# Linear attention with a butterfly FFN: k^T (x | 1) by groups of 256 features in place of x^T k with separate key sums, all keys as max(z, -b) on VectorE, first loads in smaller pieces

## The chip, the cores and the metric

The kernel runs on one core of a Trainium2 chip. The metric is device time in microseconds, from the runs of the whole program. One execution was also recorded by the hardware profiler; all rows below come from it.

## The reference, cut to what matters

```python
# x: (4, 1024, 128), W_qkv: (128, 3072), 16 heads of 64 features
q, k, v = split(x @ W_qkv)                    # each (4, 16, 1024, 64)
q = relu(q @ W_f + b_f);  k = relu(k @ W_f + b_f)
kv    = einsum('bhnd,bhne->bhde', k, v)       # sum over tokens
out   = einsum('bhnd,bhde->bhne', q, kv)
norm  = einsum('bhnd,bhd->bhn', q, k.sum(tokens))
x = layernorm(x + (out / (norm + 1e-6)) @ W_out + b_out)
h = butterfly(x @ W_exp + b_exp, up_weights)  # 512 hidden, 9 stages of 2x2 blocks
h = butterfly(gelu(h + up_bias), down_weights)
x = layernorm(x + h @ W_con + b_con + down_bias)
```

## The kernel before, in words

W_f is folded into the query and key weights and W_v into W_out, per head; the two butterflies are multiplied into W_exp and W_con once, on GpSimd and VectorE. Because v is linear in x, the sum of k v over tokens is W_v applied to the sum of k x. So the kernel never forms v: it accumulates x^T k (128 by 1024, in two PSUM banks, `kx_ps`) over the 8 token tiles of a batch, and `head_maps` (L763) turns that into one 128 by 128 map for each pair of heads.

Many products are split in high and low parts (`split`, L654): three matmuls of the type fp32r in place of one. Plain fp32 matmuls run in two passes each, so each appears as two weight loads and two matmuls in the trace.

The order of all work is written by hand in 43 slots. Every engine has one program, a loop over the slots (TensorE L879, ScalarE L1111, VectorE L1415), and waits only on semaphores. In slots 0 to 3 two token tiles are projected to keys, after that one a slot, with two query steps of 512 tokens by 128 features, and from slot 11 two steps of attention, then the up and down products of the FFN. Key and query results go through a ring of three PSUM banks (`take_ring`, L667): a bank is written again once its result has been read out.

The work around the change:
- Keys: `project_k` (L699) makes a token tile's keys in two halves of 512 features. For batches 0 and 1 a fourth matmul adds the bias row, and ScalarE reads the bank out as relu (`k_relu`, L1015). For batches 2 and 3 (`BARE`) the bias is left out, VectorE stores max(z, -b) (`k_max`, L1268), and what is missing, b times the sum over tokens, is added back at the end of a batch (`kx_end`, L1280, and `ksum_mask`, L1303). Every slot's VectorE program has the first half's eviction near its start, the second half's behind normalisation and the low parts.
- kx: `add_kx` (L727) multiplies a tile of x (weights) with its 1024 keys (moving), two fp32 matmuls of 512 columns.
- Key sums: VectorE adds the key tiles into `k_total` (`k_sum`, L1291), and `ksum` (L741) multiplies them with a column of ones, eight fp32 matmuls with one moving column, once per batch.
- The start: SP loads half of batch 0's x, the key weights in two halves, and waits for the second half before it issues more (L455 to L465). TensorE transposes weights, folds W_f (`fold_wf`, L684), ScalarE and VectorE take high and low part.
- The down butterfly on VectorE (`down_step`, L1205): two products and a sum per stage, with its coefficients loaded by SP (`load_down`, L476). The up butterfly on GpSimd (`up_step`, L573, `load_up`, L470). A load waits until the step before last has read its buffer, and everything behind it in SP's queue waits too. The bias's butterfly (`bias_row_step`, L1227) is on VectorE in slots 10 to 13, and the finished down weights are transposed in slot 13 (`ffn_weights`, L861).

Of the kernel before, what the change touches and what calls it, by code (L numbers as in the profile page):

```python
# [5 lines left out]
def postln_linear_attention_butterfly_ffn_kernel(  # L6
# [23 lines left out]

    fp32 = mybir.dt.float32
    fp32r = mybir.dt.float32r
    ALU = mybir.AluOpType
# [16 lines left out]
    ALLT = BATCH * TILES  # L50
    NORM_EPS = 1e-6
# [41 lines left out]
    KX_SLOT = {TILES * b + FIRST + 1: b for b in range(BATCH)}  # L93
# [7 lines left out]
    for b in range(BATCH):  # L101
        MAPS_SLOT[TILES * b + ATTN_AT - 2] = (b, 0)
        MAPS_SLOT[TILES * b + ATTN_AT] = (b, 1)
    XT_SLOT = {}
    for b in range(1, BATCH):
        XT_SLOT[TILES * (b - 1) + 2] = (b, 0)
        XT_SLOT[TILES * (b - 1) + 6] = (b, 1)
# [27 lines left out]
    DOWN_STEP_SLOT = {1: 0, 2: 1, 3: 2, 5: 3, 6: 4, 7: 5, 8: 6, 9: 7, 12: 8}  # L135
    PS_STEP = 3
    PS_LAST = 7

    BIAS_SLOT = {10: [0, 1], 11: [2, 3], 12: [4, 5], 13: [6]}
    BIAS_T_SLOT = 14  # L140
# [26 lines left out]

    BARE = 2 * TILES
    k_taken, taken = {}, {}
    for use in ring_of:  # L170
        if use[0] == "k" and use[1] >= BARE:
            k_taken[use] = len(k_taken) + 1
        else:
            taken[use] = len(taken) + 1
# [3 lines left out]
    desk_of = {("wq",): 0, ("wcon",): 1, ("v", 0): 2, ("v", 1): 3}  # L178
    WCON_SLOT = 0
    V_SLOT = {1: 0, 2: 1}  # L180
    for s in range(SLOTS):
        order = []
        if s in KSUM_SLOT:
            order.append(("ksum", KSUM_SLOT[s]))
        if s in ATT_T_SLOT:
            order.append(("attn", ATT_T_SLOT[s]))
        if s in MAPS_SLOT:
            order.append(("maps", *MAPS_SLOT[s]))
# [4 lines left out]
        if s == WDN_SLOT:  # L193
            order.append(("wdn",))
# [9 lines left out]
    spare_of = {}  # L204
# [13 lines left out]
    with ctx:  # L218
# [20 lines left out]
        ones = sb("ones", [128, 1])  # L239
# [3 lines left out]
        bf_h = sb("bf_h", [128, D], fp32r)  # L243
        bf_rows = sb("bf_rows", [128, CH], fp32r)
        ones_r = sb("ones_r", [128, 128], fp32r)
# [11 lines left out]
        xs = [sb(f"xs{i}", [128, TILES, C]) for i in range(XBUF)]  # L257
# [4 lines left out]
        k_total = sb("k_total", [128, HD])  # L262

        m_whole = k_total[:, :].rearrange("p (a c) -> p a c", a=PAIRS)
# [50 lines left out]
        bias_row_term = x1_flat[0:HT, 2 * CH:2 * CH + 256].rearrange("p (f n) -> p f n", f=2)  # L315
# [9 lines left out]
        s_wk = [sem(f"k_weights_half_{n}_loaded") for n in range(2)]  # L325
# [8 lines left out]
        s_xs0 = sem("first_half_of_xs_0_loaded")  # L334
# [10 lines left out]
        s_bfz = sem("bf_rows_zeroed")  # L345
        s_bfh = sem("bf_hi")
        s_bfl = sem("bf_lo")
# [6 lines left out]
        s_voa = sem("vo_copied_act")  # L354
        s_vod = sem("vo_copied_dve")
        s_xp = sem("first_x_transposed")
        s_xTh = sem("xT_hi")
# [3 lines left out]
        s_ktaken = sem("ring_bank_of_bare_k_taken")  # L361
# [15 lines left out]
        s_ks = sem("k_summed")  # L377
        s_kxt = sem("kx_half_added")
        s_kxc = sem("kx_copied")
# [36 lines left out]
        def k_summed(eng, b, t):  # L416

            eng.wait_ge(s_ks, b * (TILES - 1) + max(t, 1))

# [21 lines left out]
        def _(sp):  # L441
# [7 lines left out]
            def load_x(b, chunks, done):  # L449
                dst = xs[b][:, :, :].rearrange("p (h t) c -> p h t c", h=CHUNKS)  # L450
                sp.dma_start(dst[:, chunks, :, :], xs_view[b, :, chunks, :, :]).then_inc(done, 16)
# [32 lines left out]
            load_x(1, slice(0, CHUNKS), s_xs[1])  # L484
# [46 lines left out]
            load_down(6)  # L531
            load_down(7)
            spread(0)
# [19 lines left out]
        def _(pool):  # L553
# [6 lines left out]
            g.memset(ones_r[:, :].bitcast(fp32), 1.0)  # L560
            g.memset(bf_rows[:, :].bitcast(fp32), 0.0).then_inc(s_bfz, 1)
            g.memset(ones[:, :], 1.0)
# [43 lines left out]

            pool.wait_ge(s_wffn, 32)
            for n in range(STAGES):
                up_step(n)
            for s in range(SLOTS):  # L610
# [12 lines left out]
                if s == NO_KEYS + 2:  # L623

                    pool.wait_ge(s_kxt, 2 * TILES * BATCH)
                    last = xs[(BATCH - 1) % XBUF][:, (CHUNKS - 1) * QUADS:CHUNKS * QUADS, :]
# [19 lines left out]
        def _(pe):  # L646
# [33 lines left out]
            def transpose_weights(grp, dst):  # L680
                pe.wait_ge([s_wq, s_wq, *s_wk, s_wv, s_wv][grp], 16)
                return transpose_tiles(dst, lambda i: wqkv_raw[:, (grp * 4 + i) * 128:(grp * 4 + i + 1) * 128])

            def fold_wf(grp, dst):  # L684
                for i in range(4):
                    col = (grp * 4 + i) * 128
# [4 lines left out]
            def fold_vo(n, dst):  # L691
# [5 lines left out]
                last.then_inc(s_fold, 1)  # L697

            def project_k(kt, half):  # L699
                b, t = kt // TILES, kt % TILES  # L700
                if half == 0 and t % QUADS == 0:
# [858 lines left out]
```

## Time and profile before

| | |
|---|---|
| median of 3 runs | 328.9 us (328.84 to 331.87) |
| the profiled execution's own time | 328.99 us |
| its span, first to last instruction | 327.2 us |
| TensorE matmul busy | 311.2 us, 95% |
| VectorE busy | 249.9 us, 76% |
| ScalarE busy | 156.3 us, 48% |
| GpSimd busy | 97.1 us, 30% |
| mean granted TensorE clock | 0.991 |
| first key projection | 9.64 us |
| first key projection of slot 4 | 43.13 us |

Matmuls are pipelined and their ends are modelled, so a matmul's listed duration holds time that it shares with the next one. What a matmul costs in a stream is the step from its start to the next start. A granted clock of 1.00 is 2.4 GHz.

### The profile page before, as it was taken

How to read it: one execution, taken by the hardware profiler on the slowest of the kernel's cores; microseconds unless marked ns; L12 is line 12 of the kernel's file. 1: busy time of each engine (PE TensorE's matmuls, PEld its weight loads, DVE VectorE, ACT ScalarE, POOL GpSimd, SP SyncE). 2: the span in 40 equal slices, each digit the busy share in tenths (PEclk: the TensorE clock that was granted, in tenths of full speed). 3: DMA queues.
4: the chain of work that ended last, by engine and by line, in shares of the span. 5: the costliest groups of instructions: out<-in, count | busy, mean ns of one | idle time of the engine just before them, and what ended most of it. 6: DMA issues, size and time to landing. Idle time of an engine off the chain costs nothing.

```text
span 327.2 us, 5512 instructions
## 1 busy us (share of the span) xinstructions
PE 311.2 (95%) x2009; PEld 234.4 (72%) x2009; DVE 249.9 (76%) x501; ACT 156.3 (48%) x279; POOL 97.1 (30%) x83
## 2 busy tenths in 40 slices
PE   5999999999999899999999999999999799999893
PEld 4766677767766677667768777776797587669793
DVE  3579989978989779888890997579838953758844
ACT  3634436535733343654461556346647846431442
POOL 4059999970000002400210122002302312423513
PEclk9999999999999989999999999999999999999998
DMA  4993425556705700370064002900190174372001
GB/s 140 311 327 128 134 75 184 189 201 148 175 2 136 151 0 2 103 160 0 5 156 105 0 35 68 195 0 32 20 229 16 36 167 94 93 159 75 1 34 64
DMA packets 19762, 33.95 MB, mean 104 GB/s; under 512 B 3960, under 2 KB 6680, under 8 KB 19736
## 3 DMA queue, kind: packets, MB, share of 16 engines
q1 hardware_dynamic: 19432, 33.54, 38.9%
q8 instruction: 16, 0.26, 0.3%
q10 hardware_dynamic: 304, 0.07, 0.1%
q14 instruction: 10, 0.08, 0.1%
HBM read 31.24 MB, written 2.36 MB: 103 GB/s over the span
## 4 chain that ended last, share of the span: by engine, by line
PE 76%; DVE 14%; issue 4%; ACT 2%; DMA 1%; POOL 1%; SPq 0%; POOLq 0%; DVEq 0%; ACTq 0%
PE ring L651 28%; PE kx_ps L738 14%; PE spare_ps L841 7%; PE attn_ps L651 7%; PE ring L758 4%; PE desk L772 3%; DVE qn L1335 2%; PE desk L660 2%; PE ring L718 2%; PE desk L747 2%; DVE k_total L1301 1%; DVE qn_l L1203 1%; DVE stats L1344 1%; DMA q<-in_L_attn_W_qkv_dram 1%; DVE k L1275 1%
## 5 line engine op out<-in xcount | busy, mean ns | idle before, releaser
L599 POOL TENSOR_TENSOR rstd<-var_eps,minus_half 128x4 f32<-128x4 f32 x14 | 19.3, 1381 | 176.9 <-DVE var_eps L1350 176.9
L1029 ACT ACTIVATE q<-ring,bf_col 128x512 f32<-128x512 f32 x64 | 43.9, 685 | 46.4 <-PE ring L651 45.6
L738 PE MATMUL kx_ps<-k,xs 128*128 128x512 f32 x128 | 60.3, 594 | 0.0
L1335 DVE TENSOR_TENSOR qn<-q,recips 128x512 f32<-128x512 f32 x64 | 43.5, 719 | 2.8 <-DMA recips<-recip_rows 2.8
L1013 ACT ACTIVATE qn_h<-qn 128x512 fp32r<-128x512 f32 x48 | 29.5, 625 | 27.5 <-DVE qn L1335 27.5
L582 POOL TENSOR_TENSOR y<-hid,y_up 128x512 f32<-128x512 f32 x18 | 32.8, 1843 | 15.9 <-DMA hid<-in_L_ffn_up_weights_dram 14.9
L738 PEld LDWEIGHTS kx_ps<-k,xs 128*128 128x128 f32 x128 | 24.2, 191 | 18.0 <-issue 15.4
L1301 DVE TENSOR_TENSOR k_total<-k_total,k 128x1024 f32<-128x1024 f32 x24 | 36.5, 1520 | 0.5 <-ACT k L1020 0.3
L1203 DVE TENSOR_TENSOR qn_l<-qn,qn_h 128x512 fp32r<-128x512 f32 x48 | 33.4, 704 | 2.9 <-ACT qn_h L1013 2.7
L651 PE MATMUL ring<-xT_h,wq_h 128*128 128x512 f32 x64 | 35.6, 556 | 0.0
L1275 DVE TENSOR_TENSOR k<-ring,bf_minus 128x512 f32<-128x512 f32 x32 | 21.9, 685 | 13.7 <-PE ring L651 13.7
L651 PE MATMUL ring<-wk_h,xT_h 128*128 128x512 f32 x64 | 29.6, 463 | 0.5 <-issue 0.5
L1092 ACT ACTIVATE hid<-ring,bup_col 128x512 f32<-128x512 f32 x28 | 19.2, 686 | 22.6 <-PE ring L651 22.5
L1020 ACT ACTIVATE k<-ring 128x512 f32<-128x512 f32 x32 | 19.1, 597 | 18.1 <-PE ring L718 18.1
L841 PE MATMUL spare_ps<-wdn,hid 128*128 128x128 f32 x224 | 26.7, 276 | 0.0
L841 PEld LDWEIGHTS spare_ps<-wdn,hid 128*128 128x128 f32 x224 | 26.0, 192 | 1.0 <-issue 0.8
L651 PE MATMUL ring<-wk_h,xT_l 128*128 128x512 f32 x64 | 25.5, 399 | 0.0
L651 PE MATMUL ring<-wk_l,xT_h 128*128 128x512 f32 x64 | 25.5, 399 | 0.0
L651 PE MATMUL ring<-xT_h,wq_l 128*128 128x512 f32 x64 | 25.4, 398 | 0.0
L651 PE MATMUL ring<-xT_l,wq_h 128*128 128x512 f32 x64 | 25.4, 397 | 0.0
L595 POOL TENSOR_TENSOR y<-x,rows 128x512 f32<-128x512 f32 (+1 forms) x9 | 14.9, 1657 | 22.6 <-ACT x L1083 17.1
L651 PE MATMUL attn_ps<-qn_h,m_h 128*128 128x512 f32 x48 | 19.9, 414 | 0.3 <-DVE qn_l L1203 0.3
(174 smaller groups left out, 580.6 us busy)
## 6 DMA issues: line engine op xcount, KB each, us to landing
recips<-recip_rows SPq DMA_DIRECT2D x64, 256.0 KB, 5.4
hid<-in_L_ffn_up_weights_dram SPq DMA_DIRECT2D x9, 512.0 KB, 4.2
x<-_L_ffn_down_weights_dram SPq DMA_DIRECT2D x9, 512.0 KB, 6.7
out_dram<-y SPq DMA_DIRECT2D x7, 256.0 KB, 2.0
xs<-in_L_attn_x_dram SPq DMA_DIRECT2D x3, 512.0 KB, 6.1
q<-in_L_attn_W_qkv_dram SPq DMA_DIRECT2D x2, 512.0 KB, 4.5
xs<-in_L_attn_x_dram SPq DMA_DIRECT2D x2, 256.0 KB, 2.7
q<-in_L_attn_W_qkv_dram SPq DMA_DIRECT2D x2, 256.0 KB, 3.9
```

What stands on the lines that cost most here:

```text
L582: g.tensor_tensor(term_up[f].rearrange("p (hi j lo) -> p hi j lo", j=2, lo=lo), w[:, :, :, :, f], yv[:, :, f:f + 1, :].to_broadcast([128, ...
L599: g.tensor_tensor(rstd[i][:, :], var_eps[i][:, :], minus_half[:, :].to_broadcast([128, QUADS]), ALU.pow).then_inc(s_rs[i], 1)
L651: last = t_.matmul(dst, lhsT, rhs, start=start and n == 0, stop=stop and n == len(pairs) - 1)
L738: t_.matmul(kx_ps[half], xs[b % XBUF][:, t, :], k[kt % KRING][:, half * CH:(half + 1) * CH], start=t == 0, stop=t == TILES - 1).then_inc(s ...
L841: last = t_.matmul(dst, hid[:, j, i * 128:(i + 1) * 128], wdn[:, j, :], start=j == 0, stop=j == HT - 1)
L1013: a_.activation(dst, src, ACT.Copy).then_inc(done, 1)
L1029: a_.activation(q[:, i % QRING, :], bank(("q", i))[:, :], ACT.Relu, bias=bf_col[:, :])\
L1092: a_.activation(hid[:, i, :], bank(("up", f))[:, :], ACT.Gelu, bias=bup_col[:, i:i + 1])\
L1203: v.tensor_tensor(dst, src, high.bitcast(fp32), ALU.subtract).then_inc(done, 1)
L1275: v.tensor_tensor(k[kt % KRING][:, half * CH:(half + 1) * CH].rearrange("p (h d) -> p h d", d=D), bank(("k", kt, half))[:, :].rearrange("p ...
L1301: v.tensor_tensor(k_total[:, :], k_total[:, :], k[kt % KRING][:, :], ALU.add).then_inc(s_ks, 1)
L1335: v.tensor_tensor(qn[:, a % NRING, :], q[:, a % QRING, :], recips[:, a % PAIRS // RC, a % RC, :], ALU.mult).then_inc(s_qn, 1)
```

## The change

- kx turns round. A key unit is no longer a token tile with 1024 features but a group of 256 features for a chunk of four token tiles; a half is two of these tiles. `project_k` makes it in twelve matmuls of 256 columns where six of 512 stood, without the bias matmul for any batch. `add_kx` uses the keys as weights and a tile of x with a 129th column of ones as the moving side: eight fp32 matmuls of 129 columns per unit. The sums over tokens of the keys come out in the 129th column. `k_sum`, `k_total` and `ksum` go.
- A finished group is copied by ScalarE (`kx_copy(b, g)`, sixteen times 128 by 258), TensorE transposes it back in halves of a batch (`transpose_kx`), and `kx_end` adds the bias term per half.
- VectorE evicts all keys as max(z, -b); ScalarE evicts none. The sum over x is taken for all batches; for batch 0 VectorE sums the first x banks, and the first `add_kx` waits for that sum.
- The second chunk of a batch's x^T is needed earlier; its transposes move.
- First loads: half of batch 0's first x chunk, 256 key features, the other half of x; SP waits for the 256 features, then loads the rest of the keys' weights in two pieces. Other x loads are issued per chunk. The later `load_up`, `load_down` and x loads change their order.
- The bias's butterfly moves from VectorE to GpSimd, behind the up butterfly. Several PSUM copies move from VectorE to ScalarE. The down steps move to slots 5 to 12, the first spread over slots 2 to 4.

```diff
+    KXE_SLOT = {(TILES * b + 2 * g - 1 if b else g + 2): (b, g) for b in range(BATCH) for g in range(GROUPS)}
+    KXT_SLOT = {FIRST: (0, 0), FIRST + 2: (0, 1), TILES + FIRST: (1, 0), TILES + 6: (1, 1)}
+    for b in range(2, BATCH):
+        KXT_SLOT[TILES * b + 2] = (b, 0)
+        KXT_SLOT[TILES * b + 6] = (b, 1)
...
-    DOWN_STEP_SLOT = {1: 0, 2: 1, 3: 2, 5: 3, 6: 4, 7: 5, 8: 6, 9: 7, 12: 8}
+    DOWN_STEP_SLOT = {n + 4: n for n in range(1, STAGES)}
...
-            load_x(0, slice(0, 1), s_xs0)
-            for half in range(2):
-                cols = slice(HD + half * CH, HD + (half + 1) * CH)
-                sp.dma_start(wqkv_raw[:, cols], W_qkv[:, cols]).then_inc(s_wk[half], 16)
-
-            sp.wait_ge(s_wk[1], 16)
-            load_x(0, slice(1, 2), s_xs[0])
+            sp.dma_start(xs[0][:, 0:2, 0:C], xs_view[0, :, 0, 0:2, :]).then_inc(s_xs0[0], 16)
+            load_wk(0, slice(HD, HD + 256))
+            sp.dma_start(xs[0][:, 2:4, 0:C], xs_view[0, :, 0, 2:4, :]).then_inc(s_xs0[1], 16)
+
+            sp.wait_ge(s_wk[0], 16)
+            load_x(0, [1], s_xs[0])
+            load_wk(1, slice(HD + 256, HD + CH))
+            load_wk(2, slice(HD + CH, HD + 2 * CH))
...
             load_up(2)
             load_up(3)
+            load_up(4)
+            load_up(5)
+            for b in range(2, BATCH):
+                load_x(b, range(CHUNKS), s_xs[b])
             load_down(2)
-            load_up(4)
-            load_down(3)
-            load_up(5)
             load_up(6)
-            load_down(4)
             load_up(7)
             load_up(8)
-            for b in range(2, BATCH):
-                load_x(b, slice(0, CHUNKS), s_xs[b])
+            load_down(3)
+            load_down(4)
             load_down(5)
             load_down(6)
+            spread(0)
             load_down(7)
-            spread(0)
             load_down(8)
...
+            for b in range(XBUF):
+                g.memset(xs[b][:, :, C:C1], 1.0).then_inc(s_xones, 1)
...
+            pool.wait_ge(s_up, 3 * STAGES)
+            for st in range(LOCAL):
+                bias_row_step(st)
...
             def project_k(kt, half):
...
+                cols = slice(g * 256, (g + 1) * 256)
+                for i in range(2):
+                    t = QUADS * c + 2 * half + i
+                    tok = slice(t * 128, (t + 1) * 128)
+                    last = split(bank(("k", kt, half))[:, i * 256:(i + 1) * 256],
+                                 (xT_h[:, b % 2, tok], xT_l[:, b % 2, tok]), (wk_h[:, cols], wk_l[:, cols]))
+                last.then_inc(s_made, 1)
...
             def add_kx(kt):
...
+                b, g, c = kt // TILES, kt % TILES // 2, kt % 2
+                if kt == 0:
+                    pe.wait_ge(s_xones, XBUF)
+
+                    pe.wait_ge(s_xpart, 1)
...
+                if c == 0 and GROUPS * b + g >= 2:
+                    pe.wait_ge(s_kxe, GROUPS * b + g - 1)
                 emptied(pe, ("k", kt, 1))
                 for half in range(2):
-                    t_.matmul(kx_ps[half], xs[b % XBUF][:, t, :], k[kt % KRING][:, half * CH:(half + 1) * CH],
-                              start=t == 0, stop=t == TILES - 1).then_inc(s_kxt, 1)
-
-            def ksum(b):
...
+                    for i in range(2):
+                        for j in range(2):
+                            col = half * CH + i * 256 + j * 128
+
+                            last = t_.matmul(kx_ps[g % 2][:, j * C1:(j + 1) * C1], k[kt % KRING][:, col:col + 128],
+                                             xs[b % XBUF][:, QUADS * c + 2 * half + i, :],
+                                             start=c == 0 and half == 0 and i == 0 and j == 0,
+                                             stop=c == 1 and half == 1 and i == 1 and j == 1)
+                    last.then_inc(s_kxt, 1)
+
+            def transpose_kx(b, half):
+                take_desk(("kxT", b, half))
+                pe.wait_ge(s_kxe, GROUPS * b + 2 * half + 2)
+                transpose_tiles(desk, lambda i: kxT_pairs[:, 4 * half + i, 0:C]).then_inc(s_dmade, 1)
...
-            def kx_copy(b):
-                act.wait_ge(s_kxt, 2 * TILES * (b + 1))
+            def kx_copy(b, g):
+                act.wait_ge(s_kxt, 2 * (TILES * b + 2 * (g + 1)))
...
+                if s == 0:
+                    w_lo(2, wk_l[:, 256:CH], wk_h[:, 256:CH])
...
+                for kt in k_tiles(s)[1:]:
+                    k_max(kt, 0)
+                if s == 0:
+                    v.reduce_sum(x_part[:, 0, 1:2], desk[:, :], axis=mybir.AxisListType.X).then_inc(s_dtaken, 1)
+                    v.reduce_sum(x_part[:, 0, 0:1], kx_both[:, :].rearrange("p (a n) -> p a n", a=2)[:, :, 0:256],
+                                 axis=mybir.AxisListType.XY).then_inc(s_xpart, 1)
```

## Rows read from the trace of the kernel before

**Rows 1.** The page: busy us, share of the span, instructions of an engine.
```profile
PE 311.2 (95%) x2009; PEld 234.4 (72%) x2009; DVE 249.9 (76%) x501; ACT 156.3 (48%) x279; POOL 97.1 (30%) x83
```
**Rows 2.** Stretches (start:end, length): busy us of engines, granted clock, DMA share, GB/s.
```profile
0.00:9.60 9.60, 5.26 (x28) 4.30 (x28) 3.87 (x5) 4.06 (x8) 3.54 (x16) 1.00 0.54 168
9.60:43.10 33.50, 33.46 (x143) 23.36 (x144) 27.06 (x20) 14.17 (x25) 22.74 (x12) 1.00 0.70 209
43.10:80.30 37.20, 37.20 (x218) 26.54 (x216) 33.10 (x29) 18.12 (x31) 27.66 (x16) 1.00 0.51 163
80.30:112.00 31.70, 30.19 (x196) 21.76 (x195) 27.39 (x53) 14.64 (x25) 0.00 (x0) 1.00 0.56 127
112.00:180.00 68.00, 67.37 (x426) 49.66 (x426) 53.24 (x102) 31.51 (x56) 8.68 (x8) 0.97 0.28 65
252.00:311.00 59.00, 55.27 (x445) 43.92 (x446) 41.96 (x131) 27.82 (x49) 19.59 (x16) 1.00 0.36 87
```
**Rows 3.** Chain of waits in order of time: start, us, what.
```profile
1.65 4.34 DMA q<-in_L_attn_W_qkv_dram
...
6.04 1.12 PE ring L660 x4
7.15 1.03 PE attn_ps L687 x8
8.19 0.91 PE spare_ps L687 x8
...
9.64 0.94 PE ring L651 x3
...
12.30 0.44 PE desk L660 x4
...
41.76 0.86 PE attn_ps L695 x4
...
56.08 1.68 PE desk L747 x16
...
71.94 1.72 PE kx_ps L738 x4
73.66 1.41 PE ring L651 x6
...
173.33 3.57 PE spare_ps L841 x32
```
**Rows 4.** Groups of instructions: line, form, count, busy us, mean ns, idle before.
```profile
L738 PE MATMUL kx_ps<-k,xs 128*128 128x512 f32 x128 | 60.3, 594 | 0.0
```
**Rows 5.** Timeline of TensorE in the last chunk's up products: start, us, instruction.
```profile
313.50 0.28 PE L651 MATMUL ring<-x1T_l,wup_h 128*128 128x256 f32 x1
...
314.33 0.27 PE L651 MATMUL ring<-x1T_h,wup_l 128*128 128x256 f32 x1
```
**Rows 6.** Timeline of TensorE at the end of slot 13.
```profile
110.07 1.95 PE L747 MATMUL desk<-ones,k_total 128*128 128x1 f32 x16 [1.51 <-DVE wdn L1480]
...
113.54 0.63 PE L651 MATMUL ring<-wk_h,xT_h 128*128 128x512 f32 x1
...
115.68 0.63 PE L651 MATMUL attn_ps<-qn_h,m_l 128*128 128x512 f32 x1
```
**Rows 7.** Groups of VectorE: key sums, evictions of keys, terms of down steps.
```profile
L1301 DVE TENSOR_TENSOR k_total<-k_total,k 128x1024 f32<-128x1024 f32 x24 | 36.5, 1520 | 0.5 <-ACT k L1020 0.3
...
L1275 DVE TENSOR_TENSOR k<-ring,bf_minus 128x512 f32<-128x512 f32 x32 | 21.9, 685 | 13.7 <-PE ring L651 13.7
...
L1221 DVE TENSOR_TENSOR late<-x,spare_ps 128x512 f32<-128x512 f32 x7 | 6.2, 907 | 2.1 <-DMA x<-_L_ffn_down_weights_dram 2.1
```
**Rows 8.** Timeline of SP's queue: issue of the last two up loads.
```profile
53.95 6.00 SPq L474 DMA_DIRECT2D hid<-in_L_ffn_up_weights_dram  x2
```
**Rows 9.** DMA issues: queue, count, KB each, median us to landing.
```profile
x<-_L_ffn_down_weights_dram SPq DMA_DIRECT2D x9, 512.0 KB, 6.7
```

More of the change, by code:

```diff
@@ L102, in postln_linear_attention_butterfly_ffn_kernel @@
         MAPS_SLOT[TILES * b + ATTN_AT - 2] = (b, 0)
[L103 to L107, printed above, removed]
+        MAPS_SLOT[TILES * b + ATTN_AT - (0 if b else 1)] = (b, 1)
+    XT_SLOT = {2: (1, 0), 3: (1, 1), 8: (2, 0), 11: (2, 1)}
+    for b in range(3, BATCH):
+        XT_SLOT[TILES * b - 6] = (b, 0)
+        XT_SLOT[TILES * b - 5] = (b, 1)
     ATTN_LAST = [ATTN_AT + (PAIRS // 2) * (n + 1) - 1 for n in range(ALLCH)]
@@ L255, in postln_linear_attention_butterfly_ffn_kernel @@
         minus_half = sb("minus_half", [128, 1])
-        xs = [sb(f"xs{i}", [128, TILES, C]) for i in range(XBUF)]
+        xs = [sb(f"xs{i}", [128, TILES, C1]) for i in range(XBUF)]
         xT_h = sb("xT_h", [128, 2, N], fp32r)
@@ L323, in postln_linear_attention_butterfly_ffn_kernel @@
         desk = pb("desk")
-        s_wk = [sem(f"k_weights_half_{n}_loaded") for n in range(2)]
+        s_wk = [sem(f"k_weights_part_{n}_loaded") for n in range(3)]
         s_wq = sem("q_weights_loaded")
@@ L333, in postln_linear_attention_butterfly_ffn_kernel @@
         s_xs = [sem(f"xs_{b}_loaded") for b in range(BATCH)]
-        s_xs0 = sem("first_half_of_xs_0_loaded")
+        s_xs0 = [sem(f"tiles_of_xs_0_part_{n}_loaded") for n in range(2)]
+        s_xones = sem("x_ones_made")
         s_wffn = sem("ffn_weights_loaded")
@@ L483, in _ @@
             load_down(0)
-            load_x(1, slice(0, CHUNKS), s_xs[1])
+            load_x(1, range(CHUNKS), s_xs[1])
             for h in range(2):
@@ L678, in take_half, with transpose_weights, fold_wf @@
                     pe.wait_ge(s_dn, 3 * STAGES)
[L680 to L686, printed above, removed]
+            def transpose_weights(first, n, dst):
+                for i in range(n):
+                    last = t_.transpose(dst[:, i * 128:(i + 1) * 128], wqkv_raw[:, (first + i) * 128:(first + i + 1) * 128],
+                                        ident[:, :])
+                return last
+            def fold_wf(first, n, dst):
+                for i in range(n):
+                    col = (first + i) * 128
                     last = t_.matmul(dst[:, i * 128:(i + 1) * 128], wT[:, col:col + 128], wf_diag[:, :],
@@ L716, in project_k @@
-                if kt == 0 and half == 0:
-                    pe.wait_ge(s_bfl, 1)
-                t_.matmul(dst, ones_r[:, :], bf_rows[:, :], start=False, stop=True).then_inc(s_made, 1)
+                b, g, c = kt // TILES, kt % TILES // 2, kt % 2
+                if kt < 2:
+                    if kt == 0 and half == 0:
+                        pe.wait_ge(s_x01h, 1)
+                        pe.wait_ge(s_x01l, 1)
+                    else:
+                        pe.wait_ge(s_xTh, c + 1)
+                        pe.wait_ge(s_xTl, c + 1)
+                elif g == 0 and half == 0:
+                    pe.wait_ge(s_xTh, CHUNKS * b + c + 1)
+                    pe.wait_ge(*half_taken(("x", b, c)))
@@ L1415, in _ @@
             for s in range(SLOTS):
                 if s in KSUM_SLOT:
-                    if s == min(KSUM_SLOT):
-                        dve.wait_ge(s_const, 7)
                     ksum_mask(KSUM_SLOT[s])
-                if s in KX_SLOT and TILES * KX_SLOT[s] >= BARE:
-                    kx_end(KX_SLOT[s])
                 for kt in k_tiles(s)[:1]:
-                    if kt >= BARE:
-                        k_max(kt, 0)
+                    k_max(kt, 0)
                 if s == 0:
-                    for half, fold in enumerate([spare_ps, attn_ps]):
-                        cols = slice(half * CH, (half + 1) * CH)
-                        dve.wait_ge(s_wh, 3 + half)
-                        lo(wq_l[:, cols], fold[:, :], wq_h[:, cols], s_wl)
+                    dve.wait_ge(s_xTh, 2)
```

529 lines of the change are left out of this document (256 added, 273 removed).

## The prediction

> **What bounds the kernel now.** I read the busy times first: TensorE 311.2 of 327.2 us, VectorE 249.9 [rows 1]. A busy share says little while matmuls overlap, so the next view is the table of stretches [rows 2]. The reader is to see where TensorE is idle: 4.3 us of the first 9.6, next to nothing from 9.6 to 80.3 (33.46 of 33.50, 37.20 of 37.20), 1.5 us in 80.3 to 112, 3.7 us near the end. So from the first key projection at 9.64 on, time is what TensorE's instructions cost, and what they cost net is read from the chain of waits, where a piece's length is its step to the next [rows 3]: six split matmuls of 512 columns 1.41 us (0.235 each), a token tile's four kx passes 1.72 (0.43 a pass), sixteen ksum passes 1.68, thirty-two passes of 128 columns in the down product 3.57 (0.112 a pass), four transposes 0.44.
>
> **TensorE, part by part.** (Minus is faster.)
> 1. Bias matmuls of batches 0 and 1 go: 16 tiles x 2 halves x 0.235 [rows 3] = -7.5.
> 2. ksum goes, once per batch: 4 x 1.68 [rows 3] = -6.7.
> 3. kx turns round. Before, a tile has 4 passes, 128 in all [rows 4], 1.72 a tile. After, each of the 32 key units has 8 matmuls in two passes, 16 passes, with keys as weights and 129 columns moving. No row has 129 columns. Below, the bound is ksum's pass, which moves one column: 1.68/16 = 0.105, so 1.68 a unit and -1.3 in all; above, it is the vo fold's pass of 256 columns, 0.86/4 = 0.215 [rows 3], so 3.44 a unit and +55. The nearest row by far is 128 columns: 0.1116 x 129/128 x 16 = 1.80. I take 32 x (1.80 - 1.72) = +2.6.
> The Trainium skill speaks against this edit: TensorE: Matmul & The Clock Gate, section Back-to-back issue gap, gives about 81 ns per weight-load and matmul pair at 128 columns and 131 ns at 512. By that, 32 x (16 x 81 - 4 x 131) ns is an estimated +24.7, and the sum below would be about 343. The trace disagrees: its 512-column pass takes 3.9 times its 128-column pass (0.43 against 0.112), so cutting it into four costs little.
> 4. Key projections become halves of 256 columns. The last chunk's up products have that form: 7 steps from 313.50 to 314.33 [rows 5], 0.1186 each, so 12 x 0.1186 = 1.42 against 6 x 0.235 = 1.41: +0.4 over 32 units.
> 5. kx must be transposed back, eight times four transposes: 8 x 0.44 [rows 3] = +3.5.
> TensorE together: -7.7.
>
> **The start.** The weights' second half is what the first projection hangs on: its transfer ends at 5.99 (1.65 + 4.34), then come four transposes (1.12), folds (1.03 and 0.91 for eight passes) and the copies, till 9.64 [rows 3]. After, 256 KB stand ahead of the first transposes and folds where 768 KB stood. The landing is between a third of 4.34 us and all of it, so 3.1 to 5.99; I take half, 3.8, and 2.8 us more for two transposes, four fold passes and half-size copies, so a first projection near 6.6: -3.0. It is not all won. Six weight tiles are folded later, among the projections: 6 x 0.11 + 12 x 0.112 = +2.0. And the first add_kx now waits for VectorE's sum over x, because it overwrites the bank that is summed: behind the first projection VectorE has seven instructions in order (three key evictions, two low parts, two sums), each about 0.69 by [rows 7] (the 256-wide one less), some 4.8 us plus about one for its own waits. TensorE has only three projections, ten transposes and four fold passes meanwhile, 3.7 us, so it waits about +2.0. Start together: +1.0, between -1.0 (no such wait) and +4 (the landing no earlier either, 3.0 lost).
>
> **Slot 13.** Here the kernel has its one hole in mid-course. VectorE brings the down weights late, TensorE idles 1.51 us before ksum, and then matmuls step at 0.43 (five steps from 113.54 to 115.68) [rows 6] instead of 0.235, in the stretch with a mean granted clock of 0.97 [rows 2], so part of it at 1.2 GHz, the lower of the two levels. Seven such steps cost 1.4. ksum is gone, the weights go through another bank and ScalarE copies them, the bias rows leave VectorE. I take the hole as gone: -2.9 (0 if another wait takes its place).
>
> **VectorE, and what covers it.** It loses 28 key sums; the 24 in [rows 7] are 36.5 us. It gains 32 more evictions, as the 32 there, 21.9 us, and four half-size kx_end more. In 80.3 to 112, where normalising has begun, it is busy 27.39 of 31.70 us [rows 2]; two more butterfly steps land there (each two terms of 0.9 and a sum) and four evictions, while bias rows, a copy and three key sums go. So it stays about as full, and TensorE may run ahead by three ring banks. What fails first if that cover goes is the second key eviction: it stands behind two normalisations and the butterfly term, and the next slot's first query projection needs its bank. I give such waits +1.0, from 0 to +6 (the rival below).
> ScalarE gives up 32 evictions and takes sixteen small kx copies and some others: it stays about half idle [rows 2], at nothing. GpSimd's bias rows start after the up butterfly and are due only in slot 13: nothing, and if late, TensorE waits there. On SP's queue the two later x loads move ahead and the down weights' loads behind; more and smaller issues cost it under half a us each, covered everywhere but at the start, which is in the start's bounds.
>
> **Sum.** The profiled execution took 328.99 us (span 327.2), which is 0.1 from the median of the three runs, 328.9. -7.7 + 1.0 - 2.9 + 1.0 = -8.6, so 320.4 us. Its own range runs from 317 (the -1.0 start, no waits in VectorE) to 325 (hole replaced, or start at its worse end).
>
> **Rival 1, slower: short kx passes cost more than the down product's.** The 512 passes of 129 columns are odd in count and every second result starts 129 numbers into its bank. Each ns per pass is 0.51 us. It decides from 8.6 + 3.3 us, 23 ns a pass (0.135 instead of 0.1125), to be slower by over 1%; at half of the way to the 256-column row, 0.164, it gives 347 us. Against it: passes of 128 columns and of one differ by 7 ns only, so weights and columns overlap well. Chance 0.10.
> The skill's page PSUM — Partial Sum Buffer, section Specifications (TRN2), names 8-byte cachelines and a significant slowdown for outputs that are not contiguous; these are contiguous but half of them begin inside such a line, which no row here shows.
>
> **Rival 2, little change: the wait moves to VectorE.** Every key now leaves through an engine that works in order, and butterfly step 3 stands among the evictions of slot 7. Its weights are loaded after the last up weights, whose issue waits for GpSimd and ends at 59.95 [rows 8]; a down load of 512 KB takes 6.7 us to land [rows 9], so 67. Slot 7 would begin near 59 and the term be due near 61: VectorE, and soon TensorE, would wait up to 6 us. A second such load, step 7, waits behind the first reciprocals' spread. That and a hole that stays give 320.4 + 5 + 1.5 = 327. For it: the order in the queue is fixed. Against it: GpSimd should get through faster once the key sums, two SBUF operands each, no longer run beside it. Chance 0.22.
>
> **Rival 3, faster: the start comes through whole.** No wait on the x sum, halves landing at a third, no waits in VectorE: 320.4 - 2 - 1 - 0.7 = 316.7. It needs the loads to gain what their size promises; the first loads are smaller but also more. Chance 0.13.
>
> **Numbers.** Forecast 0.55, rivals 0.10, 0.22, 0.13. Within 1% is what a measurement of this kernel can't tell from no change: 325.6 to 332.2. Faster takes the forecast, rival 3 and a small part of rival 2: 0.71. Same takes most of rival 2: 0.18. Slower, rival 1 and a little more: 0.11. The range 316 to 328.5 leaves out rival 1, the worst of 2 and the far end of 3.
>
> **What would show it.** Right: 512 kx passes at about 0.112 us; key projections in 12 steps of 0.119; no ksum and bias matmuls; first projection near 6.6 but slot 4 (43.1 before) only one or two us earlier; no hole at slot 13 and a clock of 1.00 there; after slot 20 the same distances as before, since in batches 2 and 3 ksum's 1.68 is paid back by 0.6 for kx and 0.9 for transposes. Wrong: kx passes above 0.13, or TensorE idle in slots 5 to 12 with VectorE waiting for a down load, or the first add_kx late by more than the 2 us.

## The result, and the profile after

The changed kernel takes 325.33 us in the median (323.96 to 326.08) where the kernel before takes 329.0 beside it (328.84 to 331.87): a ratio of 0.986, 95% interval 0.981 to 0.990. A second set of runs gave 323.36 against 329.81, 0.983 (0.978 to 0.988). The forecast was 320.4. So the sign was right and some 2 to 5 us of the 8.6 did not arrive (3.7 came in the first set, 6.45 in the second). The profiled execution took 323.96 us, the fastest of its four and 5.0 less than the profiled one of before; everything below that compares the two traces accounts for these 5.0.

The page of the changed kernel, first line (answers [rows 1]):

```profile
PE 302.8 (94%) x2521; PEld 268.2 (83%) x2521; DVE 218.7 (68%) x492; ACT 142.6 (44%) x267; POOL 96.0 (30%) x105
```

TensorE lost 8.4 us of busy time and VectorE 31. The table of stretches of the changed kernel, columns as in [rows 2], says where TensorE was idle instead:

```profile
0.00:9.60 9.60, 4.77 (x20) 3.93 (x21) 3.78 (x6) 2.66 (x6) 3.04 (x17) 1.00 0.59 171
9.60:43.10 33.50, 31.87 (x262) 31.29 (x262) 17.39 (x27) 8.99 (x17) 21.20 (x15) 1.00 0.75 212
43.10:80.30 37.20, 37.04 (x330) 34.17 (x329) 30.30 (x40) 12.60 (x23) 28.39 (x33) 1.00 0.42 138
80.30:112.00 31.70, 28.63 (x254) 25.29 (x253) 27.77 (x52) 12.25 (x23) 0.00 (x0) 1.00 0.65 155
112.00:180.00 68.00, 67.83 (x583) 60.93 (x582) 45.73 (x90) 34.43 (x64) 9.17 (x8) 1.00 0.29 66
```

The reader is to see two stretches. From 9.6 to 43.1 TensorE has 1.6 us idle where it had none; from 80.3 to 112 it has 3.1 where it had 1.5. The hole of slot 13 [rows 6] is gone: 112 to 180 is full (67.83 of 68.00) and its clock 1.00, not 0.97. The chain of waits of the changed kernel (start, us, what; answers [rows 3]) gives the second place, and the price of a kx unit:

```profile
37.45 1.79 PE kx_ps L770 x16
...
85.84 2.63 issue
88.47 0.93 PE attn_ps L671 x3
```

A kx unit of 16 passes takes 1.79, 0.112 a pass. TensorE stands idle for 2.63 us ahead of the first attention product, in slot 11. In the timeline further down, slot 4's first key projection comes at 44.36, where before it came at 43.13.

### The profile page after: what moved, and what is told of

It reads as the page before. It is cut to its first block, busy times and chain, and to the rows that moved or that the text cites. A ratio compares the mean times of both kernels' runs of the same rounds, so it can differ in the third digit from the quotient of the medians.

```text
span 322.1 us, 6555 instructions
## 1 busy us (share of the span) xinstructions
PE 302.8 (94%) x2521; PEld 268.2 (83%) x2521; DVE 218.7 (68%) x492; ACT 142.6 (44%) x267; POOL 96.0 (30%) x105
## 4 chain that ended last, share of the span: by engine, by line
PE 79%; DVE 8%; issue 5%; DMA 3%; ACT 2%; SPq 1%; POOL 1%; POOLq 0%; DVEq 0%; ACTq 0%
PE ring L671 30%; PE kx_ps L770 16%; PE attn_ps L671 9%; PE spare_ps L871 8%; PE ring L788 4%; PE desk L680 3%; PE desk L802 2%; DMA recips<-recip_rows 1%; PE attn_ps L709 1%; DVE qn L1375 1%; PE attn_ps L822 1%; DVE stats L1384 1%; DMA xs<-in_L_attn_x_dram 1%; DMA recip_rows<-recip 1%; PE attn_ps L828 1%
## 5 line engine op out<-in xcount | busy, mean ns | idle before, releaser
L1327 DVE TENSOR_TENSOR k<-ring,bf_minus 128x512 f32<-128x512 f32 x64 | 43.9, 687 | 46.6 <-PE ring L671 46.5
L770 PE MATMUL kx_ps<-xs,k 128*128 128x129 f32 x512 | 62.4, 275 | 1.6 <-issue 1.6
L770 PEld LDWEIGHTS kx_ps<-xs,k 128*128 128x128 f32 x512 | 61.1, 191 | 3.4 <-issue 1.8
L671 PE MATMUL ring<-wk_h,xT_h 128*128 128x256 f32 x128 | 39.3, 307 | 1.0 <-DVE wk_l L1265 1.0
L671 PE MATMUL ring<-wk_l,xT_h 128*128 128x256 f32 x128 | 36.4, 284 | 0.0
L671 PE MATMUL ring<-wk_h,xT_l 128*128 128x256 f32 x128 | 36.4, 284 | 0.0
L671 PE MATMUL ring<-xT_h,wq_h 128*128 128x512 f32 x64 | 27.7, 434 | 0.0
L671 PEld LDWEIGHTS ring<-wk_h,xT_h 128*128 128x128 f32 x128 | 24.8, 193 | 3.3 <-issue 1.6
L671 PEld LDWEIGHTS ring<-wk_l,xT_h 128*128 128x128 f32 x128 | 24.9, 194 | 1.6
L671 PEld LDWEIGHTS ring<-wk_h,xT_l 128*128 128x128 f32 x128 | 24.7, 193 | 0.0
```

Source lines behind the costliest of these rows:

```text
L671: last = t_.matmul(dst, lhsT, rhs, start=start and n == 0, stop=stop and n == len(pairs) - 1)
L770: last = t_.matmul(kx_ps[g % 2][:, j * C1:(j + 1) * C1], k[kt % KRING][:, col:col + 128], xs[b % XBUF][:, QUADS * c + 2 * half + i, :], st ...
L1327: v.tensor_tensor(k[kt % KRING][:, half * CH:(half + 1) * CH].rearrange("p (h d) -> p h d", d=D), bank(("k", kt, half))[:, :].rearrange("p ...
```

## Where the forecast's gain went, by position

The same work in both traces, changed minus before, worked out from the starts of the same matmuls in TensorE's timeline (slot 4: first key projection; slots 8, 12, 16: first matmul of the norm; end: the execution's own time). The forecast's column adds up its terms as far as that slot.

| | before | changed | difference | by the forecast |
|---|---|---|---|---|
| slot 4 | 43.13 | 44.36 | +1.2 | -2.1 |
| slot 8 | 68.17 | 66.47 | -1.7 | -4.4 |
| slot 12 | 94.18 | 95.06 | +0.9 | -5.0 |
| slot 16 | 126.84 | 123.33 | -3.5 | -8.3 |
| end | 328.99 | 323.96 | -5.0 | -8.6 |

Two stages fall short: up to slot 4 by 3.3 us, and from slot 8 to 12 by 3.2 (a gain of 0.6 was due, 2.6 were lost). The others are better than forecast (by 0.6, 1.1 and 1.2). In both short stages 0.44 us is not lost but moved: four transposes of x stand ahead of the mark in the changed kernel that stood behind it before (16 against 12 by slot 4, 24 against 20 by slot 12; 16 and 24 in both by slots 8 and 16). So the losses are 2.9 and 2.7 us, and the stages behind them are better by 0.2 and 0.7. The timeline of TensorE in the kernel before, at slot 12:

```profile
94.18 1.95 PE L758 MATMUL ring<-q,ksum_cols 128*32 128x128 f32 x64
```

The timeline of TensorE in the changed kernel (start, us, instruction, idle time before it) shows the first of the two places, and the marks of slots 4, 8 and 12:

```profile
5.45 1.06 PE L709 MATMUL attn_ps<-wf_diag,q 128*128 128x128 f32 x4
7.53 0.55 PE L671 MATMUL ring<-wk_h,xT_h 128*128 128x256 f32 x1 [1.02 <-DVE wk_l L1265]
7.88 0.42 PE L671 MATMUL ring<-wk_l,xT_h 128*128 128x256 f32 x1
8.10 0.42 PE L671 MATMUL ring<-wk_h,xT_l 128*128 128x256 f32 x1
...
12.27 0.28 PE L671 MATMUL ring<-wk_h,xT_h 128*128 128x256 f32 x1
12.39 0.28 PE L671 MATMUL ring<-wk_l,xT_h 128*128 128x256 f32 x1
...
16.00 2.02 PE L770 MATMUL kx_ps<-xs,k 128*128 128x129 f32 x16 [1.63 <-issue]
...
44.36 0.36 PE L671 MATMUL ring<-wk_h,xT_h 128*128 128x256 f32 x1
...
66.47 1.96 PE L788 MATMUL ring<-q,ksum_cols 128*32 128x128 f32 x64 [0.16 <-ACT q L1079]
...
83.84 1.09 PE L802 MATMUL desk<-vo,kx 128*64 128x128 f32 x16 [0.44 <-DVE m_l L1265]
...
95.06 1.95 PE L788 MATMUL ring<-q,ksum_cols 128*32 128x128 f32 x64
```

The first projection begins at 7.53, not at 6.6. From there matmuls step at 0.21 us until about 12, and then at 0.12 for the same shape. They take 1.8 times as long at first, as at the lower of TensorE's two levels (1.2 and 2.4 GHz), though the stretch's granted clock reads 1.00. And the first kx product comes after 1.63 us of idle time. The second place, on SP's queue and on VectorE:

```profile
55.43 17.17 SPq L481 DMA_DIRECT2D x<-_L_ffn_down_weights_dram  x4
72.65 1.82 SPq L502 DMA_DIRECT2D recip_rows<-recip  x4
```

```profile
68.80 0.95 DVE L1359 RECIPROCAL recip<-recip 128x128 f32<-128x128 f32 x1 [1.48 <-ACT recip L1117]
...
81.89 1.29 DVE L1375 TENSOR_TENSOR qn<-q,recips 128x512 f32<-128x512 f32 x2 [1.66 <-DMA recips<-recip_rows]
...
83.70 1.11 DVE L1284 TENSOR_TENSOR late<-x,spare_ps 128x512 f32<-128x512 f32 x1
...
86.53 1.11 DVE L1284 TENSOR_TENSOR attn_ps<-x,spare_ps 128x512 f32<-128x512 f32 x1
87.67 0.70 DVE L1294 TENSOR_TENSOR spare_ps<-late,attn_ps 128x512 f32<-128x512 f32 x1
```

The reciprocals are done at 69.7, but SP issues their spread at 72.65: the last of four down loads in front of it (step 6's) waits until step 4's terms have left its buffer. VectorE then idles 1.66 us for the spread, and after it has a slot's worth of work up to the sum of step 6 at 88.4. The first attention product waits for that sum, because step 6 keeps its second term in the attention bank. So there seem to be two causes in a row; the next experiments take them away one by one.

## Experiments: slot 11

The changed kernel ran again beside three variants.

> The changed kernel once more, unaltered, so that the three beside it have it on the same chip. Both theories: 324 to 326 us, a ratio of 0.983 to 0.991 to the kernel before; TensorE idle 2.6 us in slot 11 ahead of the first attention product, and the first key projections of 256 columns stepping at 0.21 us until about 12 us.

Measured: 323.36 us (323.26 to 324.36), a little below the 324 to 326 expected, with the idle time (2.64 us) in slot 11 and the slow first steps as expected. The variants of the next sections are compared with this run where nothing else is said.

**The bank.**

```diff
-    PS_LAST = 7
+    PS_LAST = 6
```

> Step 6 of the down butterfly keeps its second term in SBUF and not in the attention bank, so the first attention product waits for step 5 alone. Theory A (the 2.6 us hole of slot 11 is the wait for the attention bank, which VectorE frees late because step 6's terms and sum stand in slot 10 behind two normalisations, two low parts and an eviction): the first attention product starts by 86.0 instead of 88.5, the hole shrinks to under 0.6, the kernel is 2 to 2.6 us faster than the changed one. Theory B (the hole is the late spread of the reciprocals, which SP issues behind a down load): the product then waits for the low part of q instead, the hole stays above 1.5 and the time moves by less than 1 us.

Measured: 321.96 us (321.51 to 322.03), ratio 0.977 (0.973 to 0.982). The timeline of TensorE:

```profile
84.17 1.09 PE L802 MATMUL desk<-vo,kx 128*64 128x128 f32 x16 [0.32 <-DVE m_l L1265]
86.00 0.39 PE L671 MATMUL attn_ps<-qn_h,m_h 128*128 128x512 f32 x1
...
93.09 1.18 PE L788 MATMUL ring<-q,ksum_cols 128*32 128x128 f32 x35 [0.48 <-DVE k L1327]
```

The hole is gone and the product comes at 86.00 as theory A said, and the profiled executions differ by 2.3 us (322.03 and 324.36), but the medians by 1.4 and not by 2 to 2.6 (the slowest of its runs is still 1.2 below the fastest of the changed kernel's). VectorE is still late, and TensorE meets it again at 93.09.

**The spread.**

```diff
+        coef_dn.append(qn[:, 2:4, :].rearrange("p a n -> p (a n)"))
+        DN_BUF = [0, 1, 0, 1, 0, 1, 2, 1, 0]
...
-                if n >= 2:
+                if n >= 2 and n != 6:
                     sp.wait_ge(s_dn, 3 * n - 4)
```

> The down load of step 6 gets a coefficient buffer of its own and no wait, so the spread of the first reciprocals no longer stands behind it. It is issued near 70.0 instead of 72.65. Theory B (the late spread makes the hole): first normalisation at 80.2 instead of 81.9, hole under 0.6, 2.3 to 3 us faster than the changed kernel. Theory A (VectorE's order and the attention bank make it): VectorE gains the 1.7 us it idled ahead of the first normalisation, but the 6.5 us from there to the sum of step 6 stay, so about 1.0 to 1.5 us of hole stay and the gain is 1.3 to 2 us.

Measured: 322.37 us (322.08 to 322.87), ratio 0.979 (0.973 to 0.985). SP's queue, and the chain of waits:

```profile
70.14 1.73 SPq L504 DMA_DIRECT2D recip_rows<-recip  x4
```

```profile
85.62 1.38 issue
87.01 0.94 PE attn_ps L673 x3
```

The spread goes out at 70.14, VectorE no longer idles, and 1.38 us of the hole stay: theory A's 1.0 to 1.5. The gain, 1.0, is a little under its 1.3, and again no run overlaps with the changed kernel's.

**Both.**

> Only the two edits for slot 11 (step 6 out of the attention bank, and a coefficient buffer of its own for step 6 so that the spread goes out early). Theory A (each takes away one of two things in a row, so together they leave nothing to wait for): no idle time ahead of the first attention products, first one at 85.6 or earlier, 2.6 to 3.1 us less than the changed kernel, so 320.3 to 321 us. Theory B (they cure the same wait, and the bank alone already cured it): no better than the bank alone, 322 us.

Measured: 320.83 us (319.99 to 321.63), ratio 0.973 (0.969 to 0.978): 2.5 less than the changed kernel's 323.36, about the sum of the two alone (1.4 and 1.0). TensorE's timeline has the first attention product with no idle time before it:

```profile
85.33 0.40 PE L673 MATMUL attn_ps<-qn_h,m_h 128*128 128x512 f32 x1
```

Theory A holds: two causes in a row. The bank alone already takes away the wait ahead of this product, but only both edits leave VectorE nothing to be late with at slot 12 as well.

## Experiments: the start

**Idle transposes.**

```diff
             pe.wait_ge(s_const, 2)
+            idle_work(8)
             transpose_first_x(0)
...
+            idle_work(3)
             transpose_first_x(1)
...
             fold_wf(PAIRS, 2, attn_ps)
+            idle_work(5)
```

> Sixteen transposes of the identity into a bank not yet in use: eight before the first x tiles are there, three while the second piece of x is awaited, five behind the first folds. Nothing reads them. Theory A (the first key projections step at 0.21 us because TensorE had been idle between its first pieces of work and still ran at the lower clock): steps of 0.12 from the first projection at 7.5 on, slot 4's first projection 1.5 to 2.5 us earlier than 44.6, the kernel 1.5 to 2.5 us faster than the changed one. Theory B (the slow steps are the weight loads or the DMA traffic of the start): steps stay at 0.21 until about 12 us, and the time moves by less than 0.5 us.

Measured: 324.57 us (324.39 to 325.15), 1.2 slower than the changed kernel beside it in the median and the same in the profiled execution (324.39 and 324.36). Yet the steps are as theory A has them:

```profile
5.76 0.71 PE L903 MATMUL ring<-ident 128*128 128x128 f32 x5
6.95 0.35 PE L671 MATMUL ring<-wk_h,xT_h 128*128 128x256 f32 x1 [0.48 <-DVE wk_l L1272]
7.14 0.28 PE L671 MATMUL ring<-wk_l,xT_h 128*128 128x256 f32 x1
7.26 0.28 PE L671 MATMUL ring<-wk_h,xT_l 128*128 128x256 f32 x1
```

They step at 0.12 from the first unit on, and the norm of slot 8 begins at 64.47, not 66.87: 2.4 us won, 0.9 of it ahead of the first projection (6.95 for 7.83). The weight loads of these matmuls and the DMA traffic (163 GB/s in the first 9.6 us of both traces) are the same, so what made the steps slow is that TensorE had been idle. (The Trainium skill, TensorE: Matmul & The Clock Gate, section What's actually happening, gives 1.2 GHz as the state of an idle array and 2.4 GHz as that of a busy one; these two traces agree, 0.21 and 0.12 for 256 columns.) The chain of waits then shows the loss:

```profile
84.79 2.63 issue
87.43 1.62 PE attn_ps L671 x3
89.05 2.17 PE ring L671 x9
```

The hole of slot 11 is as long as before, and behind it three products take 1.62 and nine 2.17, where the changed kernel has 0.94 and 1.40. That stretch's granted clock is 0.95. So 1.4 us go there, and 1.0 to the store of the reciprocals, which took 3.74 us to land in this run and 2.73 in the other. All four runs have a lower mean clock (0.991 to 0.995) than the changed kernel's four (0.996 to 1.000). Why the store was late and why the clock fell stays open.

**The x sum.**

```diff
             lo(xT_l[:, 0, 0:256], kx_ps[0][:, 0:256], xT_h[:, 0, 0:256], s_x01l)
+            v.reduce_sum(x_quart[:, 0:1], kx_ps[0][:, 0:256], axis=X).then_inc(s_xquart, 1)
...
-                    pe.wait_ge(s_xpart, 1)
+                    pe.wait_ge(s_xquart, 1)
+                elif kt == 2:
+                    pe.wait_ge(s_xquart, 2)
```

> Only the x sum of batch 0 in two pieces, so that the first kx product waits for a sum taken long before. Theory A (the 1.63 us TensorE idles ahead of it are the wait for that sum): the first kx product starts near 14.4 instead of 16.0, slot 4 comes 1.6 us earlier, and the time is 0 to 1.6 us less than the changed kernel's 323.4, less than 1.6 if slot 11 takes it back as it did with the idle transposes. Theory B (it waits for the evicted keys): the idle time stays above 1 us.

Measured: 322.44 us (321.81 to 325.0), ratio 0.978 (0.971 to 0.986), so 0.9 us less than the changed kernel by the medians and 1.5 by the ratios, within the intervals. TensorE's idle time ahead of the first kx product is gone:

```profile
14.77 1.95 PE L773 MATMUL kx_ps<-xs,k 128*128 128x129 f32 x16
```

It starts right behind the transposes. These come 0.56 us later than in the first trace of the changed kernel (14.34 for 13.78), as the slow steps last until 12.8 here. Slot 4 comes at 43.11 instead of 44.36, and slot 11 keeps an idle 2.47. Theory A.

**The size of the first loads.**

```diff
-            sp.dma_start(xs[0][:, 0:2, 0:C], ...
-            load_wk(0, slice(HD, HD + 256))
-            sp.dma_start(xs[0][:, 2:4, 0:C], ...
+            sp.dma_start(xs[0][:, 0:4, 0:C], ...
+            load_wk(0, slice(HD, HD + CH))
...
-            load_wk(1, slice(HD + 256, HD + CH))
```

> The first half of batch 0's x in one load of 256 KB instead of two of 128, and the first 512 columns of the key weights in one load of 256 KB instead of two of 128; all else as changed. Theory A (the forecast's step: the first projection comes earlier because less has to land before it): the first projection starts 0.6 to 1.2 us later than 7.5. Theory B (what brought it forward is that two weight tiles are transposed and folded ahead of it, not eight, and the number of loads costs what their size saves): it starts within 0.3 us of 7.5, and the time stays within 0.5 us.

Measured: 325.61 us (324.48 to 325.99), ratio 0.986 (0.979 to 0.992). The chain of waits:

```profile
1.48 3.31 DMA q<-in_L_attn_W_qkv_dram
...
8.35 1.62 PE ring L669 x6
```

The weights' transfer ends at 4.79, and the first projection starts at 8.35: 0.8 later than 7.53, and later than in each trace with the small loads and no idle transposes (7.22 to 7.83). Theory A holds, for 0.8 of the 2.1 us by which the change brought the first projection forward from 9.64; the rest was not taken apart further. The edit makes both the first x load and the first weight load larger, so the two are not told apart. In the whole time it doesn't show beyond the intervals.

**Both start edits.**

> Only the two edits for the start (idle transposes, x sum in two pieces). Theory A (slot 11 is a fixed date set by the reciprocals' spread, so what the start wins is given back there): TensorE's lead of about 4 us at slot 8 shrinks at slot 11, where idle time grows beyond 3 us or the clock falls after it, and the time is 321.5 to 324 us. Theory B (the start's gains are kept whole): 319 to 320 us.

Measured: 322.24 us (320.86 to 322.81), ratio 0.977 (0.972 to 0.983). The number is theory A's, the mechanism is not. The norm of slot 8 begins at 64.30, 2.6 earlier than in the changed kernel (the two alone gave 2.4 and 1.65; here TensorE waits 0.9 for VectorE's kx_end in slot 4). In slot 11 the chain has:

```profile
83.77 2.65 issue
86.42 0.93 PE attn_ps L673 x3
```

The hole is as long as ever and the rate behind it whole. The product comes at 86.42 instead of 88.85, so 2.4 of the 2.6 are kept, and the profiled executions differ by as much (322.01 and 324.36); the medians differ by 1.1. So slot 11 is no fixed date: SP's queue and VectorE move forward with the start. What took the gain back in the run with idle transposes alone were that run's late store (3.74 us, here 3.30) and its slow matmuls behind the hole.

## Experiments: the parts

**The bias matmuls alone.** On the kernel before:

```diff
-    BARE = 2 * TILES
+    BARE = TILES
...
-                if s == 5:
-                    act.wait_ge(s_bias, 16 * (1 + HT))
+                if s == 2:
+                    act.wait_ge(s_bfc, 32)
                     a_.activation(bf_minus[:, :], bf_row[:, :], ACT.Copy, scale=-1.0).then_inc(s_bfm, 1)
```

The second part only has ScalarE make -b in slot 2, because it is needed earlier.

> The kernel before with one part of the change: batch 1's keys too are taken as the larger of z and -b on VectorE, without bias matmuls and with the x sum added at the end, as batches 2 and 3 had it; key sums, kx, loads and order stay. Theory A (the bias term of the forecast stands alone, 16 matmuls of 0.235): 3 to 3.75 us faster than before. Theory B (VectorE has no room for 16 more evictions of 0.69 while it also sums the keys and works through the down butterfly, 33 of 37 us busy in slots 4 to 9): TensorE waits for evictions and the gain is under 1 us or a loss of up to 4.

Measured: 336.94 us (335.49 to 339.27), ratio 1.023 (1.014 to 1.032): slower by 6, past theory B's 4. Its stretch of slots 4 to 9, and what TensorE waited for (us, times, longest):

```profile
43.10:80.30 37.20, 32.47 (x181) 22.82 (x180) 33.23 (x34) 9.52 (x15) 27.16 (x16) 0.95 0.43 142
```

```profile
PE ring L651 <- DVE k L1275: 3.5, 2, 3.0
PE kx_ps L738 <- issue: 3.2, 1, 3.2
...
PE ring L758 <- DVE k L1275: 1.6, 2, 1.3
```

Inside the change the bias matmuls of two batches went, 7.5 us of steps by the forecast's price, and TensorE never waits for a key eviction in the changed kernel's trace; on the kernel before, the same edit for one batch costs 6. So this part of the change has no price of its own: it depends on what else VectorE does. That it is the key sums which make the difference fits the two traces but was not tested alone.

**The width of a kx pass.**

```diff
+                            w = C1 if c == 0 and half == 0 and i == 0 else C
...
-                                             xs[b % XBUF][:, QUADS * c + 2 * half + i, :],
+                                             xs[b % XBUF][:, QUADS * c + 2 * half + i, 0:w],
```

> The changed kernel with 128 columns moving in 448 of the 512 kx passes, the ones column only in the first pass of a pair's group, so the key sums are left short. Theory A (a pass costs its columns, and the odd count and the results that begin 129 numbers into the bank cost nothing): a unit of 16 passes takes 1.77 instead of 1.79 us, the time falls by 0.4 us or less. Theory B (the odd width or the start inside a line costs something): a unit takes 1.70 or less and the time falls by 2 us or more.

Measured: 325.51 us in one run. Units in its chain of waits:

```profile
21.22 1.79 PE kx_ps L771 x16
25.75 1.78 PE kx_ps L771 x16
```

Within 0.01 us of 129 columns: theory A for the price; a unit does not even fall to 1.77. Half of the results still begin 129 numbers into the bank, as the output's places are unchanged, so this run tells only of the odd count; that the place costs nothing is told by the price itself, 0.112 as in the down product. The time is above the changed kernel's because the clock of 80.3 to 112 was 0.95 here too: behind the hole of 2.63, three products took 1.62 and nine 2.08.

**All four edits together.**

> Four edits together on the changed kernel: step 6 keeps out of the attention bank, step 6's coefficients have a buffer of their own so that the spread goes out early, sixteen idle transposes at the start, and batch 0's x sum in two pieces, the first taken in VectorE's idle time before the first projection. Theory A (start and slot 11 were the two places where the forecast's gain went, and in the run with idle transposes alone the 2.4 us won by slot 8 were lost in slot 11 because the reciprocals did not come earlier and the clock fell after the hole): the parts add, 2.4 for the clock, 1.6 for the x sum, 1.5 to 2.6 for slot 11, so 317 to 319 us. Theory B (VectorE bounds the first twelve slots as a whole): what is won at the start returns as other waits by slot 12, and the time is 321 to 322, as with the bank or the spread alone.

Measured: 317.86 us (316.71 to 318.36), ratio 0.962 (0.956 to 0.969): theory A. The chain and the stretch:

```profile
81.95 0.90 PE ring L675 x6
82.85 0.69 PE attn_ps L675 x3
83.54 1.41 PE ring L675 x9
```

```profile
80.30:112.00 31.70, 31.70 (x272) 28.11 (x271) 28.97 (x55) 13.82 (x25) 0.00 (x0) 1.00 0.47 113
```

No idle time is left in slot 11, and the first attention product comes at 82.85, against 88.47. By their medians the start's edits are worth 3.0 us on top of slot 11's (320.83 to 317.86), and 1.1 without them; by the ratios to the runs of the kernel before beside each, 3.6 and 1.8.

> The four edits together, with three idle transposes behind the first folds instead of five: in the run with five, TensorE was still busy with them until 7.57, while the first projection's operands were there by 7.4. Theory A (the other idle transposes are enough to have TensorE at the higher clock by the first projection): first projection by 7.4 in steps of 0.12, 317 to 318 us, as with five or 0.2 better. Theory B (the clock needs these too): the first projections step at 0.21 again, and the time is 319 to 320 us.

Measured: 318.08 us (317.26 to 318.36), ratio 0.965 (0.961 to 0.968), the first projection at 6.84 in steps of 0.12. Theory A, with no gain over five. This version and the one before it beat both kernels.

## Why the prediction was right, and where it was not

- **TensorE's terms were right.** kx: 1.79 a unit where 1.80 was taken, so +2.2 for +2.6; key halves step at 0.118 (0.71 for six); eight kx transposes at 0.44; bias matmuls and ksum gone. Busy time fell by 8.4 us, where 7.7 were forecast, but that also holds the slow steps of slot 13 before and of the start after. Rival 1 is out: 0.112 a pass, with 0.135 needed. The rule of the Trainium skill (TensorE: Matmul & The Clock Gate, section Back-to-back issue gap), by which the time would have come to an estimated 343 us, does not hold for these passes: a unit of 16 takes 1.79 us where the estimate had 1.30, and the four wide passes that it replaces took 1.72 where the estimate had 0.52.
- **Slot 13's hole, -2.9: right.** TensorE is busy 67.83 of 68.00 us there, at a clock of 1.00; slots 12 to 16 gained 4.4 us where 3.3 were due, 0.44 of it the transposes that had moved ahead.
- **The start, +1.0: mis-sized.** It is +3.9 (2.9 short by slot 4), just inside its bound of +4. The step that failed is "a first projection near 6.6 ... Start together": it priced every matmul of the new start at full rate. Of the 3.9, the first projection makes -2.1 where -3.0 was taken, the later folds 2.0 as taken, and the wait for the x sum 1.63 for 2.0 (without it slot 4 came 1.25 earlier). The rest, 2.4, had no term: it is the rate. In the chain of waits the first three key halves and the six transposes among them take 5.25 us, where the later ones of their kind take 2.79. Before, transposes and folds run from 6.04 to 9.10 and the last eight folds take 0.91, full rate already, when the first projection comes [rows 3]; after, there are ten short passes with gaps between them, and the slow steps last until 12. Idle transposes give 1.5 of it back behind the first projection, and 0.9 ahead of it. The first projection was 0.9 late for two reasons. The step counted 256 KB ahead of the first folds, but TensorE's program has the transposes of the second 128 KB piece of x ahead of them too, and this piece ends at 4.9, after the weights. And the four fold passes take 0.87 (0.45 at full rate).
- **VectorE waits, +1.0: mis-sized**, +3.1 (2.63 and 0.44 ahead of the second maps) inside the bounds of 0 to 6, and another 1.4 in runs where the clock falls behind the hole. (By the table the stage lost 0.6 more than this idle time explains; that was not taken apart.) The step took the second key eviction for what fails first. It is the attention bank's release, and SP's queue: rival 2 had a down load waiting behind the spread, and neither it nor the step had the spread waiting behind a down load that itself waits for VectorE. Rival 2's own place did not come: the ten down terms into late waited 0.0. What it set against itself held: GpSimd got through faster (second line before, third after), and the last up load's issue ended at 53.2 instead of 59.95. In the variant with the bias matmuls alone, which keeps the key sums, GpSimd's step took 1.88 us; that they are the cause was not tested alone.

```profile
L1284 DVE TENSOR_TENSOR late<-x,spare_ps 128x512 f32<-128x512 f32 x10 | 9.5, 945 | 0.0
L586 POOL TENSOR_TENSOR y_up<-y 128x512 f32<-128x512 f32 x9 | 17.6, 1960 | 0.7
L586 POOL TENSOR_TENSOR y_up<-y 128x512 f32<-128x512 f32 x9 | 12.2, 1354 | 0.7
```

- **VectorE as cover** was right in kind: 64 evictions (43.9 us) went through without TensorE waiting for one, and the variant with evictions and key sums together shows waits for them (3.5 and 1.6 us). That VectorE lost 31 us of work also shows behind slot 16, where 1.2 us more came than forecast: the kernel before waits three times for VectorE ahead of its head maps (1.1 us in all), the changed one once (0.5).
- **Rival 3** asked for the start without loss: the four edits come nearest to it, 317.86 where 316.7 was worked out.

Of the prediction's signs, the price of a kx pass, the steps of 0.119, the missing hole and the clock of slot 13 came as written. Two did not: slot 4 came 1.2 us later, not one or two earlier, and the distances after slot 20 are not the same as before (2.9 us ahead there, 5.0 at the end). And TensorE did stand idle in slots 5 to 12 behind a down load, only that VectorE waited for the spread behind it and not for the load.

With slot 11 mended the time is 320.83 us beside 329.66, 8.8 less, close to the sum of 8.6, but that is in part luck. The variant still has the start's loss: its norm of slot 12 begins 2.4 us earlier than before, where 5.0 were forecast, and it gains 5.9 behind slot 12, where 3.6 were forecast. What the forecast took at nothing there (fewer waits for VectorE, the moved transposes) accounts for a part of these 2.3; the rest stays open.

## What to carry to other kernels

When work is taken from in front of TensorE's first products, ask what rate it will have there: work that was removed may have been what brought it to full rate. When loads are reordered on a queue, list for each of them what it waits for and everything that then stands behind it, also what is not a load. And a bank or buffer that two engines share in turn has a date at which it must be free: when work moves between slots, look up who holds it then.

## What the runs showed of the hardware that was not expected

- At the start the granted clock reads 1.00 while 256-column matmuls step at 0.21; with sixteen more transposes ahead they step at 0.12. The granted clock does not tell of it, the steps do.
- Six traces have the hole of slot 11 at 2.62 to 2.65 us. In four of them the three products behind it take 0.93 or 0.94, in two (idle transposes alone, and 128 columns moving) 1.62, with a granted clock of 0.95 in the stretch. So 1.4 us come or go with the same work around the hole; what decides it stays open. The changed kernel's first four runs, 323.96 to 326.08, have mean clocks of 0.996, 0.991, 0.991 and 0.987, in that order.
